# One common order of 63 steps between two attentions, rearranged

## The chip, the cores and the metric

The kernel runs on one core of a Trainium2 chip. A core has four compute engines that run side by side, each working through its own instruction queue in order: TensorE (PE, matrix products and transposes through the array), VectorE (DVE), ScalarE (ACT) and GpSimd (POOL). SyncE (SP) issues the DMAs. The engines meet only at semaphores: an instruction waits until a counter has reached a value, and everything behind it in its queue waits too. The metric is the device time of one execution in microseconds.

## The reference, cut to what matters

Two layers over 1024 tokens of width 512. Each computes `x + attention(norm(x)) * silu(ffn(norm(x)))`; the first layer's attention has 8 heads of 8 channels, its feed-forward part is a base product with eight low-rank experts. What concerns this case is the passage from the first layer's attention to the second's:

```
s  = attention_0(xn)            # ends in out @ Wo_w.T + Wo_b, per tile of 128 tokens
x  = x + s * g                  # g = silu(ffn_0(xn)), already there
xn = _layernorm(x)              # over the 512 channels
q = (xn @ Wq.T)                 # 32 heads of 128, 8 groups of 4 heads
k = (xn @ Wk.T); v = (xn @ Wv.T)   # 8 key/value heads of 128
q, k = _rmsnorm(q, q_norm_w), _rmsnorm(k, k_norm_w)
scores = q k^T / sqrt(128) + alibi bias, causal; softmax; @ v; @ Wo.T
```

## The kernel before

Tokens are handled in eight tiles of 128 rows. Products in full precision are made from three products of half-split operands (`mm3`, L2035 to L2039: high by high, high by low, low by high), so each operand of TensorE comes as a high part, mostly written by ScalarE, and a low part, mostly written by VectorE (what is left after the high part is taken away).

The program has three stages that matter here. First comes a loop of 32 steps of the first attention. Into its last steps tiles 0 to 3 of the next stage are woven (`EARLY = 4`). Then comes the stretch that this case is about, written out as a list of 63 steps, `TAIL` (L322 to L328). Then comes a long loop of 64 slots of the second attention (`slot_items`), which goes through the key/value groups one by one.

A step of `TAIL` is a pair (kind, tile). Four engines walk the same list, each doing its own share of a step (TensorE L2334, ScalarE L1322, VectorE L1815, GpSimd L1053); a step in which an engine has no share is passed over. SyncE doesn't walk it. The kinds are:

- `OS` and `OH`: TensorE transposes the attention sums of a tile (L2223), VectorE divides them (`normalise`, L1680 to L1691); TensorE transposes the result (L2230), ScalarE writes its high half (L1245), VectorE its low half (`low_on`, L1700).
- `WO`: TensorE makes the first layer's output product into bank WB (three matmuls, L2239 to L2243), VectorE multiplies it with the gate (L1708), GpSimd adds x (`add_x`, L1034). The sum is what SyncE stores (L784).
- `LS` and `LA`: statistics of the new x on VectorE (L1494, L1495), reciprocal root on GpSimd (`rstd`, L934 to L940), and the normalised tile on ScalarE (`apply_act`, L1320).
- `XT`: TensorE transposes the normalised tile (L2058), ScalarE and VectorE write the halves (L1137, L1507).
- `KV`: key/value product of a tile for group 0 (twelve matmuls of 256 columns, into the S banks), ScalarE squares the keys (L1338) and copies the values (L1340), GpSimd makes the inverse root (`inverse_k`, L962, L963). `VL` is VectorE's low half of the values (L1796), `SC` VectorE's scaling of the keys (L1806), `KT` the transpose of the keys (L2316) with its halves (L1304, L1777).
- `PQ`, `SQ`, `QT`: query projection of a row tile (twelve matmuls of 512 columns; `PQ` 0 goes to bank VB, `PQ` 1 to bank WB), sums of squares on ScalarE (L1279), inverse roots on GpSimd (`inverse_rms`, L955 to L957), scaling on VectorE (L1764), transposes (L2311) and halves (L1300, L1772).
- `S0`: the four score products of the first query tile, VectorE's bias and maximum (L1784), ScalarE's exponentials (L1310).

Semaphore values are computed from the list. The transposes of `OS`, `OH`, `XT`, `KT` and `QT` alternate between the two halves of bank T, so each waits until VectorE has emptied the one before last (`ring`). `KV` of tiles 4 to 7 waits until `VL` and `SC` of the tile four before are done (`KV_FREE`). `KV` of tiles 4 to 7 and `PQ` 1 wait for VectorE's half of `XT`; `OH` waits for its `OS` on VectorE; `QT` 1 waits for all sixteen `VL` and `SC` steps. The first work of slot 0 of the long loop is another query projection into WB, which waits for `SQ` 1, then the scores of its first head, which wait for every `KT` and `QT` of the list on VectorE.

Of the kernel before, what the change touches and what calls it, by code (L numbers as in the profile page):

```python
# [16 lines left out]
NT, KT = TOK // P, D // P  # L17
# [22 lines left out]
QT = 10240  # L40
# [180 lines left out]
def slot_items(n):  # L221
# [65 lines left out]
    else:  # L287
# [31 lines left out]
T_OUT = 16  # L319


TAIL = [("KV", 0), ("OS", 4), ("KV", 1), ("VL", 0), ("OH", 4), ("OS", 5), ("KV", 2), ("VL", 1), ("WO", 4),  # L322
# [6 lines left out]
KV_FREE = {}  # L329
for _x in TAIL:  # L330
    if _x[0] in ("VL", "SC"):
# [8 lines left out]
T_AT = {}  # L340
for _x in TAIL:
    if _x[0] in ("OS", "OH", "XT", "KT", "QT"):
# [125 lines left out]
def program(nc, x, w0, w1, codes, absmax, lora, consts, rows, rel, out):  # L468
    with ExitStack() as ctx:
# [451 lines left out]
        def _(pool):  # L921
# [8 lines left out]
            def rstd(t, bias=False):  # L930

                k = t % NT
                hold(pool, var_ready, t + 1, p_passed)
                ch.link(e.tensor_scalar(VE[:, k:k + 1], MV[:, k, 1:2], 1.0, LN_EPS, ALU.mult, ALU.add))  # L934
                root = e.tensor_tensor(RSTD[:, k:k + 1], VE[:, k:k + 1], C[:, C_EXP:C_EXP + 1], ALU.pow)
                if bias:

                    ch.link(root)
                    ch.link(e.tensor_tensor(NB[:, k:k + 1], MV[:, k, 0:1], RSTD[:, k:k + 1], ALU.mult))
                    root = e.tensor_scalar(NB[:, k:k + 1], NB[:, k:k + 1], -1.0, 0.0, ALU.mult, ALU.add)  # L940
                root.then_inc(rstd_ready, 1)
# [95 lines left out]
            for x in range(NBX):  # L1037
# [4 lines left out]
                for it in unit_items(x):  # L1042
# [8 lines left out]
                    elif it[0] == "LS":  # L1051
                        rstd(NT + it[1])
            for kind, t in TAIL:  # L1053
                if kind == "WO":
# [75 lines left out]
        def _(act):  # L1130
# [190 lines left out]

            for x in TAIL:  # L1322
                kind, b = x
# [163 lines left out]
        def _(dve):  # L1487
# [326 lines left out]

            for x in TAIL:  # L1815
                kind, t = x
# [215 lines left out]
        def _(pe):  # L2032
# [300 lines left out]

            for x in TAIL:  # L2334
                kind, b = x
# [301 lines left out]
```

## Time and profile before

| | us |
|---|---|
| median of 3 runs | 1408.86 (1408.39 to 1411.47) |
| the profiled execution's own time | 1408.48 |
| its span, first to last instruction | 1406.7 |
| mean granted TensorE clock, share of full speed | 0.989 |
| busy in the span: TensorE, VectorE, ScalarE, GpSimd | 1344.7, 931.9, 880.0, 660.8 |

The profile tells for each engine how long it was busy, and for each instruction what ended the idle time before it. Times of single instructions are counted from the span's start. Ends of matmuls are modelled, so that neighbouring matmuls overlap in the listing; the distance from start to start is what one costs in a row of them. Instructions are told by line: in this stretch L2037 to L2039 are products (bank S for `KV`, VB and WB for `PQ`), L2058 is `XT`, L2223 `OS`, L2230 `OH`, L2239 the start of `WO`, L2311 `QT` and L2316 `KT`.

### The profile page before, as it was taken

Reading aid. Unit: us, or ns where it says so; the run is one execution under the profiler, and the core shown is the slowest. Engines: PE = TensorE matmul, PEld = TensorE weight load, DVE = VectorE, ACT = ScalarE, POOL = GpSimd, SP = SyncE. Lnnn points to the kernel's source line nnn. Section 1 sums busy time; section 2 is a strip of 40 time slices with the busy share of each in tenths; the row PEclk is TensorE's granted clock in tenths of the full one; section 3 lists DMA queues with packets and bytes.
Section 4 is the critical chain, followed back from the end, with each engine's and each line's share of the span. In section 5 each row is a group of like instructions: output and inputs, shape, how many; then the busy total and the mean of one; then the engine's idle time right before and its main releaser. Section 6 shows DMA issues by size and latency. Waiting matters only on the chain. (4 is left out here: it accounts for less than half of the span.)

```text
span 1406.7 us, 21472 instructions
## 1 busy us (share of the span) xinstructions
PE 1344.7 (96%) x7350; PEld 1078.3 (77%) x7350; DVE 931.9 (66%) x1659; ACT 880.0 (63%) x2167; POOL 660.8 (47%) x988
## 2 busy tenths in 40 slices
PE   6898987999999999999999999999999999999997
PEld 5543345788888888888888888888888887778886
DVE  5766555667776777767677767777676777676433
ACT  6255564667776777667677767776676766663211
POOL 5233266445465555545454645555454545443311
PEclk9999999899999999999999999999999999999999
DMA  4100032102010110102020101101020202033110
GB/s 162 53 1 1 0 106 71 31 1 61 27 51 11 52 56 22 47 16 77 2 61 27 51 11 52 61 16 51 12 77 1 62 11 50 5 95 120 36 61 30
DMA packets 36028, 61.02 MB, mean 43 GB/s; under 512 B 9200, under 2 KB 13424, under 8 KB 35920
## 3 DMA queue, kind: packets, MB, share of 16 engines
q1 hardware_dynamic: 35920, 59.66, 13.6%
q8 instruction: 59, 0.97, 0.3%
q14 instruction: 49, 0.40, 0.1%
HBM read 49.68 MB, written 9.96 MB: 42 GB/s over the span
## 5 line engine op out<-in xcount | busy, mean ns | idle before, releaser
L947 POOL TENSOR_TENSOR RI<-SM,C 128x1 f32<-128x1 f32 x256 | 151.8, 593 | 410.3 <-ACT PB L1310 410.1
L1791 DVE TENSOR_TENSOR R<-T,R 128x512 fp32r<-128x512 f32 x288 | 198.8, 691 | 115.4 <-ACT R L1383 105.0
L1784 DVE CUSTOM_DVE_ANT_0 PB<-S,REL,SLC 128x128 f32<-128x128 f32 (+7 forms) x256 | 204.6, 813 | 82.9 <-PE S L2039 79.9
L1310 ACT ACTIVATE PB<-PB,NM 128x128 f32<-128x128 f32 (+7 forms) x256 | 198.2, 774 | 45.5 <-DVE NM L1784 44.7
L1383 ACT ACTIVATE R<-T 128x512 fp32r<-128x512 f32 x288 | 171.3, 596 | 81.1 <-PE T L2428 78.0
L948 POOL TENSOR_SCALAR PB<-PB,RI 128x128 f32<-128x128 f32 (+7 forms) x256 | 209.7, 819 | 25.2
L2428 PE MATMUL T<-C,PB 128*128 128x128 f32 x1152 | 176.0, 276 | 7.6 <-DVE R L1791 3.3
L2428 PEld LDWEIGHTS T<-C,PB 128*128 128x128 f32 x1152 | 135.7, 141 | 37.6 <-DVE R L1791 13.9
L1370 ACT ACTIVATE DQ<-DQ 128x704 f32<-128x704 int32 x128 | 97.5, 785 | 78.4 <-DVE DQ L1865 76.4
L2037 PE MATMUL WB<-R,XT 128*128 128x512 f32 (+1 forms) x268 | 105.1, 392 | 0.0
L2039 PE MATMUL WB<-R,XT 128*128 128x512 f32 (+1 forms) x268 | 103.9, 388 | 0.0
L2038 PE MATMUL WB<-R,XT 128*128 128x512 f32 (+1 forms) x268 | 103.7, 387 | 0.0
L2037 PE MATMUL T<-R 128*128 128x512 f32 x256 | 101.8, 398 | 1.0 <-DVE R L1791 1.0
L2039 PE MATMUL T<-R 128*128 128x512 f32 x256 | 100.4, 392 | 0.0
L2038 PE MATMUL T<-R 128*128 128x512 f32 x256 | 100.0, 391 | 0.0
L2037 PE MATMUL S<-R 128*128 128x512 f32 (+3 forms) x252 | 92.8, 368 | 0.9 <-DVE NM L1784 0.9
L1211 ACT ACTIVATE PB<-S 128x1024 f32<-128x1024 f32 x64 | 65.1, 1023 | 43.8 <-PE S L2186 43.5
L2039 PE MATMUL S<-R 128*128 128x512 f32 (+3 forms) x252 | 89.7, 356 | 0.0
L1279 ACT ACTIVATE JUNK<-WB 128x128 bf16<-128x128 f32 x252 | 65.5, 273 | 33.5 <-PE WB L2039 33.5
L1865 DVE TENSOR_TENSOR DQ<-DQ 128x704 f32<-128x704 f32 x96 | 86.4, 900 | 0.0
L2038 PE MATMUL S<-R 128*128 128x512 f32 (+3 forms) x240 | 84.9, 354 | 0.0
L1653 DVE TENSOR_REDUCE MH<-T 128x2 f32<-128x1024 f32 x48 | 58.8, 1225 | 35.5 <-PE T L2170 35.5
(311 smaller groups left out, 3501.9 us busy)
## 6 DMA issues: line engine op xcount, KB each, us to landing
RAW<-w SPq DMA_DIRECT2D x85, 256.0 KB, 2.7
DQ<-codes SPq DMA_DIRECT2D x16, 352.0 KB, 4.0
DQ<-absmax SPq DMA_DIRECT2D x16, 352.0 KB, 2.9
dequantised<-DQ SPq DMA_DIRECT2D x16, 352.0 KB, 4.1
PB<-dequantised SPq DMA_DIRECT2D x5, 512.0 KB, 3.5
PB<-x SPq DMA_DIRECT2D x8, 256.0 KB, 4.7
PB<-x_scratch SPq DMA_DIRECT2D x8, 256.0 KB, 3.7
out<-PB SPq DMA_DIRECT2D x8, 256.0 KB, 2.0
```

Source lines behind the costliest of these rows:

```text
L947: ch.link(e.tensor_tensor(RI[:, k:k + 1], SM[:, k:k + 1], C[:, C_EXP + 5:C_EXP + 6], ALU.pow))
L948: e.tensor_scalar(pb(m, a, 0, L), pb(m, a, 0, L), RI[:, k:k + 1], scale, ALU.mult, ALU.mult).then_inc(probs_ready, 1)
L1310: e.activation(pb(m, a, 0, L), pb(m, a, 0, L), ACT.Exp, scale=-1.0, bias=NM[:, k:k + 1], accum_out=SM[:, k:k + 1]).then_inc(exp_done, 1)
L1370: e.activation(DQ[:, to, :], CODES, ACT.Copy, scale=sc, bias=bi).then_inc(line, 1)
L1383: e.activation(r(PT + AT[i, ("PV", kb)] % 3 * 1024, 512), T[AT[known, it] % 2][:, :], ACT.Copy).then_inc(t_act, 1)
L1784: e.tensor_tensor_reduce(out=pb(m, a, 0, L), in0=bank[:, 0:L], in1=REL[:, TOK - L:TOK], scale=SLC[:, a:a + 1], scalar=3.0e38, op0=ALU.add, ...
L1791: e.tensor_tensor(r(o + 512, 512), bank[:, :], rf(o, 512), ALU.subtract).then_inc(t_free, 1)
L1865: e.tensor_tensor(DQ[:, b, :], DQ[:, b, :], DQ[:, 3, :], op).then_inc(line_used, 1)
L2037: e.matmul(dst, lh, rh, start=start, stop=False)
L2038: e.matmul(dst, lh, rl, start=False, stop=False)
L2039: return e.matmul(dst, ll, rh, start=False, stop=stop)
L2428: last = e.transpose(bank[:, a * P:(a + 1) * P], pb(i, a, kb * P, (kb + 1) * P), IDENT)
```

## The change

The list `TAIL` gets another order. It holds the same 63 steps. Nothing else is edited; the semaphore values and the places in bank T follow from the list.

```diff
-TAIL = [("KV", 0), ("OS", 4), ("KV", 1), ("VL", 0), ("OH", 4), ("OS", 5), ("KV", 2), ("VL", 1), ("WO", 4),
-        ("OH", 5), ("OS", 6), ("KV", 3), ("SC", 0), ("LS", 4), ("WO", 5), ("OH", 6), ("OS", 7), ("VL", 2),
-        ("SC", 1), ("KT", 0), ("LA", 4), ("LS", 5), ("WO", 6), ("OH", 7), ("SC", 2), ("KT", 1), ("XT", 4),
-        ("LA", 5), ("LS", 6), ("WO", 7), ("PQ", 0), ("VL", 3), ("SC", 3), ("KT", 2), ("XT", 5), ("LA", 6),
-        ("LS", 7), ("KV", 4), ("KT", 3), ("XT", 6), ("VL", 4), ("SQ", 0), ("LA", 7), ("KV", 5), ("SC", 4),
-        ("QT", 0), ("XT", 7), ("VL", 5), ("KT", 4), ("KV", 6), ("SC", 5), ("PQ", 1), ("KT", 5), ("KV", 7),
-        ("VL", 6), ("SC", 6), ("KT", 6), ("S0", 0), ("VL", 7), ("SC", 7), ("KT", 7), ("SQ", 1), ("QT", 1)]
+TAIL = [("OS", 4), ("OS", 5), ("OH", 4), ("KV", 0), ("WO", 4), ("OH", 5), ("OS", 6), ("SC", 0), ("KV", 1),
+        ("WO", 5), ("OH", 6), ("LS", 4), ("OS", 7), ("SC", 1), ("KV", 2), ("WO", 6), ("OH", 7), ("KT", 0),
+        ("LS", 5), ("VL", 0), ("VL", 1), ("LA", 4), ("KV", 3), ("KT", 1), ("WO", 7), ("VL", 2), ("LS", 6),
+        ("LA", 5), ("SC", 2), ("XT", 4), ("LS", 7), ("PQ", 0), ("XT", 5), ("VL", 3), ("KT", 2), ("SC", 3),
+        ("LA", 6), ("KV", 4), ("XT", 6), ("SQ", 0), ("SC", 4), ("KT", 3), ("LA", 7), ("KV", 5), ("VL", 4),
+        ("XT", 7), ("VL", 5), ("KV", 6), ("VL", 6), ("SC", 5), ("QT", 0), ("SC", 6), ("KT", 4), ("PQ", 1),
+        ("KT", 5), ("KT", 6), ("KV", 7), ("S0", 0), ("SQ", 1), ("SC", 7), ("VL", 7), ("QT", 1), ("KT", 7)]
```

## Rows read from the trace of the kernel before

**Rows 1.** The page, part 1: busy us (share of the span) xinstructions
```profile
PE 1344.7 (96%) x7350; PEld 1078.3 (77%) x7350; DVE 931.9 (66%) x1659; ACT 880.0 (63%) x2167; POOL 660.8 (47%) x988
```

**Rows 2.** Windows: length, busy time by engine, PEclk, DMA share, GB/s
```profile
204.30:245.40 41.10, 31.52 (x193) 26.12 (x189) 21.28 (x68) 18.92 (x72) 22.87 (x49) 0.93 0.25 85
218.00:222.70 4.70, 4.54 (x14) 3.37 (x15) 3.16 (x9) 1.30 (x2) 3.16 (x9) 0.64 0.15 56
243.00:250.00 7.00, 5.45 (x16) 4.44 (x16) 1.70 (x3) 1.05 (x2) 3.50 (x8) 0.51 0.22 67
...
265.00:1150.00 885.00, 881.86 (x4998) 750.11 (x4998) 626.36 (x1148) 629.65 (x1694) 454.60 (x728) 1.00 0.12 37
```

**Rows 3.** Timeline of PE, later part: start, length, operation, idle before
```profile
218.16 0.66 PE L2058 MATMUL T<-C,PB 128*128 128x128 f32 x4 [1.95 <-DVE R L1700]
...
233.85 0.40 PE L2037 MATMUL WB<-R,XT 128*128 128x512 f32 x1
...
236.61 0.27 PE L2316 MATMUL T<-C,L0S 128*128 128x128 f32 x1
...
244.62 1.09 PE L2311 MATMUL T<-C,QN 128*128 128x128 f32 x4 [1.55 <-issue]
245.36 0.78 PE L2037 MATMUL WB<-R,XT 128*128 128x512 f32 x1
...
250.36 0.40 PE L2037 MATMUL S<-R 128*128 128x512 f32 x1
...
259.87 0.80 PE L2311 MATMUL T<-C,QN 128*128 128x128 f32 x4 [1.99 <-DVE QN L1764]
```

**Rows 4.** Timeline of ACT
```profile
204.48 0.60 ACT L1232 ACTIVATE DQ<-VB 128x512 f32<-128x512 f32 x1 [0.70 <-PE VB L2199]
...
215.22 0.80 ACT L1320 ACTIVATE PB<-PB,NB,RSTD 128x512 f32<-128x512 f32 x1
...
224.29 0.28 ACT L1279 ACTIVATE JUNK<-VB 128x128 bf16<-128x128 f32 x1 [4.13 <-PE VB L2039]
```

**Rows 5.** Timeline of DVE
```profile
206.36 0.21 DVE L1680 RECIPROCAL RS<-T 128x8 f32<-128x8 f32 x1 [1.85 <-PE T L2223]
...
206.87 0.28 DVE L1796 TENSOR_TENSOR R<-S,R 128x128 fp32r<-128x128 f32 x1
...
210.62 0.69 DVE L1708 SCALAR_TENSOR_TENSOR G<-WB,G 128x512 f32<-128x512 f32 x1 [1.12 <-PE WB L2243]
...
243.78 0.68 DVE L1764 TENSOR_TENSOR QN<-WB,INV 128x512 f32<-128x512 f32 x1
```

**Rows 6.** Timeline of PE, the first 7 us of the stretch
```profile
203.34 1.06 PE L2199 MATMUL VB<-PB,L0S 128*32 128x512 f32 x8 [1.86 <-ACT PB L1211]
204.34 0.38 PE L2037 MATMUL S<-R,XT 128*128 128x256 f32 x1
...
205.87 0.38 PE L2223 MATMUL T<-C,DQ 128*128 128x128 f32 x2
...
209.36 0.49 PE L2239 MATMUL WB<-R 64*128 64x512 f32 x1
...
210.35 0.27 PE L2230 MATMUL T<-C,ON 128*128 128x128 f32 x1
```

**Rows 7.** Timeline of POOL, in the stretch and in the long loop
```profile
211.40 1.28 POOL L1034 TENSOR_TENSOR PB<-PB,G 128x512 f32<-128x512 f32 x1 [0.65 <-DVE G L1708]
...
213.71 0.19 POOL L934 TENSOR_SCALAR VE<-MV 128x1 f32<-128x1 f32 x1
...
215.04 1.28 POOL L1034 TENSOR_TENSOR PB<-PB,G 128x512 f32<-128x512 f32 x1
...
225.79 1.03 POOL L956 TENSOR_TENSOR SQC<-SQB,C 128x4 f32<-128x4 f32 x1
...
323.50 0.91 POOL L948 TENSOR_SCALAR PB<-PB,RI 128x768 f32<-128x768 f32 x1
...
325.01 1.29 POOL L948 TENSOR_SCALAR PB<-PB,RI 128x768 f32<-128x768 f32 x1
```

## The prediction, made before the changed kernel ran

> **What bounds the kernel now.** I read the page first: TensorE is busy 96% of the span, far above the others [rows 1]. Then the windows. In the long loop it is busy 881.9 of 885.0 us, so whatever reaches that loop earlier ends earlier by the same amount. In the stretch of the 63 steps it is busy only 31.5 of 41.1 us, its granted clock is 0.93 in the mean, in two parts of it (218 to 222.7, 243 to 250) it is 0.64 and 0.51, so that there TensorE ran at the lower of its two levels, 1.2 against 2.4 GHz, most or all of the time [rows 2]. No other engine is busy more than 23 us of the 41. So the stretch is bound by chains between in-order queues, not by an engine. Last I read the timelines for what ends each pause. TensorE's pauses add up to 41.1 - 31.5 = 9.6 us. The longest is 1.95 us ahead of `XT` 4: it waits for VectorE's `OH` 7 half, which stood behind a statistics step that waited for GpSimd. At the end it pauses 1.55 us ahead of `QT` 1, and the next query projection, at the half clock, runs from 245.36 to 250.36, 5.00 us, where the same twelve matmuls took 236.61 - 233.85 = 2.76 at the full one [rows 3]. ScalarE stood 4.13 us at `PQ` 0's squares with later key transposes queued behind them [rows 4].
>
> **The change, part by part.** No instruction, DMA or byte is added or removed; only waits and order differ. SyncE's queue isn't reordered; its stores follow GpSimd's additions, which come earlier or within 0.3 us of before for the last tiles. So the cost is found by walking the four queues in the new order, with each step's length from the rows and about 0.05 to 0.15 us from one engine to the next (transpose listed as ending at 206.25, division at 206.36) [rows 5, 6]. I walk to one point: the first score product of slot 0, 250.36 before [rows 3].
>
> *The front.* The list now opens with `OS`, `OS`, `OH` where two key/value products stood. The last values product ends at 204.40, and before, `KV` 0 began at 204.34, hiding the copy of the sums [rows 6]. Now TensorE must wait for that copy, which ends at 205.08 [rows 4]; `OS` 4 starts at 205.15. VectorE's division follows at 205.64 and is done about 0.6 later (its three instructions take 0.51 to the next one's start [rows 5], and the last ends a little after that), so `OH` 4 runs at 206.35 and `KV` 0 at 206.45, 2.1 us later than before. That is the loss. In exchange `WO` 4 starts at 206.45 + 1.53 = 208.0 and not at 209.36; a `KV` costs 205.87 - 204.34 = 1.53, a `WO` 210.35 - 209.36 = 0.99 [rows 6]. The gate (0.69) is done at 210.0 [rows 5] and GpSimd's first addition runs at 210.1, not 211.4 [rows 7].
>
> *The middle, TensorE.* From there it finds everything ready: `KV` 1 to 210.8, `WO` 5 to 211.9, `KV` 2 to 213.7, `WO` 6 to 214.7, `OH` 7 at 214.74, just as its division ends, `KV` 3 to 216.5, `WO` 7 to 217.6, `XT` 4 to 218.0, `PQ` 0 (2.76) to 220.7, `XT` 5 to 221.1, `KV` 4 to 222.9. The 1.95 us pause goes, since `XT` 4's bank is emptied by `OH` 7 and `KT` at about 216.2, before `LS` 5 in VectorE's queue.
>
> *The middle, GpSimd.* This is the next chain. An addition costs 1.28, the root of `LS` with its three small steps 215.04 - 213.71 = 1.33 [rows 7], a key root about 0.8 (estimated: an `LS` root without two of its small steps). `LS` 4 can start when the second addition ends, 214.3, and from there GpSimd never rests: `LS` 4, root, addition 6 to 217.7, `LS` 5 to 219.1, root, addition 7 to 221.1, `LS` 6 to 222.6, `LS` 7 to 223.9, `PQ` 0's roots (1.03 for the long one, 1.6 in all [rows 7]) to 225.4. ScalarE applies each in 0.80 [rows 4]. So `XT` 6 waits until 223.55 (0.45 of listed pause), and `XT` 7, whose ScalarE step stands behind `KT` 3's half, until 225.85 (0.15). `SQ` 0 ends at 226.2, long before `QT` 0 is due at 227.8. ScalarE's 4.13 us wait goes too: when it comes to `PQ` 0's squares, after `XT` 4, it waits at most 0.5.
>
> *The end.* `KV` 6 to 227.8, `QT` 0, `PQ` 1 to 231.1, `KV` 7 to 232.9, two first scores to 233.6, the other two 0.35 later each as VectorE frees their banks. VectorE's four maxima, of 128 columns like the 0.28 of a `VL` [rows 5] and with a result to read back, end at about 235.1, `SQ` 1 (0.68 [rows 5]) at 235.8, `SC` 7 and `VL` 7 at 236.3. `QT` 1 waits for these: listed pause 1.95, start 236.4. `KT` 7 now stands last and is ready for 0.1. Slot 0's projection starts at 237.0, where 245.36 stood, and at the full clock its score product starts at 237.0 + 2.76 = 239.8. GpSimd's first probabilities are ready at 238.5 and all at 241.5, before the transposes that need them (244).
>
> *The sum.* 250.36 - 239.8 = 10.6 us. It comes out again another way. New listed pauses: 0.75 + 0.70 at the front, 0.1 at `KT` 2, 0.45, 0.15, 0.2 at the scores and 1.95, together 4.3 against 9.6: 5.3 less. Some seven pauses fewer also spare the end of a matmul that is otherwise overlapped (listed 0.40, but 2.76/12 = 0.23 from start to start [rows 3], so 0.16 each): 1.1. The half clock between 218 and 222.7, 0.36 of 4.7 us below full and so 0.72 of it at half [rows 2], cost some 1.7, and with the small steps up to 1.9, and the one at slot 0's projection 2.24. 5.3 + 1.1 + 1.9 + 2.2 = 10.5.
>
> *The clock, the unknown term.* In the trace it was low behind the 1.95 us pause and around the 1.55 us one [rows 2, 3]. The new order has two such places: the front (1.86 us before the last values product [rows 6], then 0.75 and 0.70) and the end (0.2, then 1.95). Bounds: nothing where it stays up; 2.24 each where it falls and stays down over a whole query projection, as before [rows 3]. I take one fall of the two, 1.9: 10.5 - 1.9 = 8.6. The later pause of 1.99 us in slot 0 [rows 3] is taken as it was. The Trainium skill speaks against the change at the front: "TensorE: Matmul & The Clock Gate", section on what is actually happening, has the engine throttled by default and the full rate only granted for recent activity, so a front of short transposes and waits should lose it. By that rule both falls come and the gain is about 6.8; the trace agrees that the clock falls behind clustered pauses, yet after the 1.86 us pause ahead of the last values product `KV` 0 ran at 0.13 us a matmul, the full rate [rows 6].
>
> *Against the profiled execution.* Its own time, 1408.48, is 0.38 below the median of 1408.86. 1408.5 - 8.6 = 1399.9; I forecast 1400.0.
>
> **The rivals.** *A: GpSimd becomes the bound (20%).* It works back to back from 214.3 to 225.4. The same scaling in the long loop took 0.91 and, 1.5 us later, 1.29 [rows 7]: 0.38 more. If each of the seven long steps of the chain grows so, `LA` 6, `LA` 7 and all after come 2.5 us later; with one clock fall the gain is 6.1, and with both, 4.2: 1402.4 to 1404.3. For: the stretch packs VectorE denser beside it. Against: both additions listed in the stretch took 1.28 [rows 7]. The Trainium skill, "SBUF — State Buffer", section "Who interferes with whom", has a VectorE instruction with two SBUF inputs block a GpSimd one that reads SBUF. Nearly all VectorE steps here read PSUM for one input, so by that rule little would be added; the row agrees.
>
> *B: the clock stays up more than I grant (12%).* Neither fall comes, or the transposes behind slot 0's 1.99 us pause, listed at 0.80 and so probably at the half clock [rows 3], run with what follows at the full one, worth up to 1.7 more as the fall above: gain 10.5 to 12.2, 1396.3 to 1398.
>
> *C: slower, by the half clock (5%).* The clock falls at the front, at 205, and the short pauses keep it down to the end of the stretch. At the half clock a 512-column matmul costs 0.42 (5.00/12) against 0.23, so each us of full-speed work costs 0.8 more. The 10.5 us gain is used up from 13 us of such work on; over all of the stretch's 27 us (31.5 less overlapped ends and slow parts) it is 22 - 10.5: 1420. For: three pauses in 5 us at the front. Against: both falls in the stretch ended once TensorE issued without pause, and from 206.45 to 221.1 it has none.
>
> *D: no change (5%).* The waits that follow from the list hold the ends where they were, or slot 0 waits for something else that doesn't move (its chunks of weights, the probabilities): within 2.8 us. Against: the weights for slot 1 are issued after GpSimd's last low halves, which move with the rest.
>
> **The numbers.** Forecast 58%, own range 1398.0 to 1402.4. With 12% below that, 20% above in A, 5% no change, 5% slower. The range for 8 in 10 is 1396.3 to 1404.3. A measurement of this kernel can tell about 0.2%, 2.8 us: faster 0.90, same 0.05, slower 0.05.
>
> **What would show it right or wrong.** In the new profile: two short pauses ahead of L2223 and L2230 at 204.4 to 206.4; the first L1034 of the stretch near 210.1; no pause over 0.5 us on TensorE from 207 to 223; GpSimd without rest from 214 to 225; a pause of about 2 us ahead of the last L2311; slot 0's first score product at 239.8 to 242. The walk is wrong if that product comes later than 244 with the clock at full, or if TensorE pauses over 1 us in the middle. The gain should stand whole at the end of the span: if the score product comes 8 us earlier and the end doesn't, the claim about the long loop is what failed.

## The result, and the profile after

The changed kernel takes 1398.25 us (median of 4 executions, 1396.86 to 1399.49) against 1410.03 for the kernel before in the same rounds: ratio 0.9917, 95% interval 0.9900 to 0.9935. The forecast was 1400.0, range 1396.3 to 1404.3. Over the executions whose clock was recorded the kernel before has a mean of 1410.5 (60 executions; two more, of 2189.89 and 2638.86, are far out of line and left out) and the changed one 1399.6 (10): 10.9 us, give or take 2.2. The profiled execution took 1399.04, its span is 1397.2.

The profile's page, first part, then windows of the stretch: length, busy time by engine, PEclk (the clock granted to TensorE, as a share of full speed), DMA share, GB/s. The first window runs from the last values product to slot 0's query projection and answers to the first of [rows 2]:

```profile
PE 1342.4 (96%) x7350; PEld 1075.9 (77%) x7350; DVE 933.1 (67%) x1659; ACT 880.2 (63%) x2167; POOL 661.8 (47%) x988
```

```profile
205.50:239.90 34.40, 30.12 (x193) 25.64 (x189) 21.20 (x67) 18.42 (x71) 20.40 (x44) 0.95 0.25 90
206.50:210.50 4.00, 3.57 (x18) 3.07 (x18) 1.38 (x7) 0.28 (x1) 0.00 (x0) 0.57 0.45 182
210.50:239.90 29.40, 26.36 (x172) 22.44 (x172) 19.63 (x59) 17.54 (x69) 20.40 (x44) 1.00 0.20 67
...
255.00:1150.00 895.00, 891.98 (x5044) 758.03 (x5043) 635.39 (x1163) 637.11 (x1712) 461.57 (x738) 1.00 0.12 37
```

The stretch is 34.4 us and not 41.1, with the same 193 matmuls in the window; TensorE's listed pauses are 34.4 - 30.1 = 4.3 us and not 9.6. The half clock (1.2 GHz) comes once, at the front, between 206.5 and 210.5. In the long loop TensorE is as full as before.

TensorE's timeline, with all its pauses from the last values product to slot 0's transposes (it answers to [rows 3, 6]):

```profile
204.53 1.06 PE L2199 MATMUL VB<-PB,L0S 128*32 128x512 f32 x8 [1.77 <-ACT PB L1211]
206.41 0.78 PE L2223 MATMUL T<-C,DQ 128*128 128x128 f32 x4 [0.81 <-ACT DQ L1232]
207.62 0.45 PE L2230 MATMUL T<-C,ON 128*128 128x128 f32 x1 [0.43 <-DVE ON L1691]
207.75 0.55 PE L2037 MATMUL S<-R,XT 128*128 128x256 f32 x1
...
210.42 0.50 PE L2239 MATMUL WB<-R 64*128 64x512 f32 x1
...
226.25 0.63 PE L2058 MATMUL T<-C,PB 128*128 128x128 f32 x4 [0.62 <-DVE R L1777]
...
228.62 0.63 PE L2058 MATMUL T<-C,PB 128*128 128x128 f32 x4 [0.20 <-ACT PB L1320]
...
236.60 0.33 PE L2037 MATMUL S<-R 128*128 128x128 f32 x1 [0.27 <-DVE NM L1784]
...
239.34 0.66 PE L2311 MATMUL T<-C,QN 128*128 128x128 f32 x4 [1.85 <-DVE R L1796]
...
239.86 0.47 PE L2037 MATMUL WB<-R,XT 128*128 128x512 f32 x1
...
242.70 0.39 PE L2037 MATMUL S<-R 128*128 128x512 f32 x1
...
252.19 0.66 PE L2311 MATMUL T<-C,QN 128*128 128x128 f32 x4 [1.99 <-DVE QN L1764]
```

The 1.95 us pause ahead of `XT` 4 is gone, and so are those ahead of `QT` 0 and of four key transposes, of 0.80 to 1.22 us (three of these five show below, in the kernel with the old rest of the list). The row at 226.25 names VectorE's half of `KT` 2, which ends at 226.16; `XT` 6 needs ScalarE's `LA` 6, which ends at 226.11 (row below). Slot 0's projection takes 242.70 - 239.86 = 2.84 us (5.00 before). From the end of the last values product (205.59; 204.40 before) to slot 0's first score product it is now 37.11 us and was 45.96. The span shrank by 9.5: 8.85 here, 1.84 behind it (1156.34 us from that score product to the end before, 1154.50 now), less 1.19 ahead of the stretch, which the list doesn't touch.

Of the 1.84 us, 1.59 lie in slot 0. Its 1.99 us pause is there in both, but before, the clock fell at it (0.84 from 259.8 to 270.4 us, 1.00 in the 9 us ahead of that) and now it doesn't (1.00 from 252.1 to 262.7). TensorE's timeline at the next group of such transposes (`L2311`) behind that pause, of the kernel before, then of the changed one:

```profile
278.92 0.60 PE L2311 MATMUL T<-C,QN 128*128 128x128 f32 x4
```

```profile
269.67 0.60 PE L2311 MATMUL T<-C,QN 128*128 128x128 f32 x4
```

From slot 0's first score product that is 278.92 - 250.36 = 28.56 us before and 269.67 - 242.70 = 26.97 now; I call this place "past slot 0's fall".

### The profile page after: what moved, and what is told of

Its sections match the earlier page's. It is cut to its first block and busy times, and to the rows that moved or that the text cites. A ratio compares the mean times of both kernels' runs of the same rounds, so it can differ in the third digit from the quotient of the medians.

```text
span 1397.2 us, 21472 instructions
## 1 busy us (share of the span) xinstructions
PE 1342.4 (96%) x7350; PEld 1075.9 (77%) x7350; DVE 933.1 (67%) x1659; ACT 880.2 (63%) x2167; POOL 661.8 (47%) x988
## 5 line engine op out<-in xcount | busy, mean ns | idle before, releaser
L2428 PEld LDWEIGHTS T<-C,PB 128*128 128x128 f32 x1152 | 135.7, 141 | 37.8 <-DVE R L1791 13.6
L2037 PE MATMUL WB<-R,XT 128*128 128x512 f32 (+1 forms) x268 | 103.9, 388 | 0.0
L2039 PE MATMUL WB<-R,XT 128*128 128x512 f32 (+1 forms) x268 | 103.0, 384 | 0.0
L2038 PE MATMUL WB<-R,XT 128*128 128x512 f32 (+1 forms) x268 | 102.6, 383 | 0.0
```

The source lines that it names most:

```text
L2037: e.matmul(dst, lh, rh, start=start, stop=False)
L2038: e.matmul(dst, lh, rl, start=False, stop=False)
L2039: return e.matmul(dst, ll, rh, start=False, stop=stop)
L2428: last = e.transpose(bank[:, a * P:(a + 1) * P], pb(i, a, kb * P, (kb + 1) * P), IDENT)
```

## The experiments

All are timed in rounds with the kernel before. I write "equal clock" for what is left of a difference in time when the clock's part is taken out, as below. To compare places in the trace I use distances from the end of the last values product (`L2199`), since that end itself lies between 202.6 and 210.5 us from one execution to the next. In us, by the profiled execution of each kernel:

| | first `WO` | `PQ` 0 | `QT` 1 | first score of slot 0 | past slot 0's fall |
|---|---|---|---|---|---|
| before | 4.96 | 15.71 | 40.22 | 45.96 | 74.52 |
| changed | 4.83 | 14.72 | 33.75 | 37.11 | 64.08 |
| changed, once more | 3.75 | 13.64 | 32.67 | 37.50 | 64.51 |
| old head, new rest | 4.96 | 15.71 | 35.63 | 40.44 | 67.39 |
| new head, old rest | 4.85 | 14.77 | 38.41 | 43.41 | 70.39 |
| end alone | 4.96 | 15.44 | 39.27 | 44.14 | 71.08 |
| `LS` 5 later | 5.91 | 15.25 | 40.72 | 46.61 | 75.15 |
| front filled | 3.75 | 13.63 | 32.66 | 37.33 | 64.28 |
| both filled | 3.74 | 13.63 | 32.70 | 36.04 | 64.57 |
| `KV` 0 first | 4.38 | 13.44 | 32.46 | 37.21 | 64.17 |
| the same, end filled | 4.37 | 13.46 | 32.47 | 35.81 | 64.37 |
| `PQ` 1 early | 4.35 | 13.44 | 34.87 | 40.07 | 67.05 |
| before, filled | 4.97 | 15.35 | 38.66 | 41.88 | 70.43 |

The last column stands behind every place where these profiles show the half clock in or just after the stretch, so it holds what the order and its falls of the clock give together: 74.52 - 64.08 = 10.4 us for the change (10.0 in its repeat).

Every execution has its mean granted clock. Over all of them one line fits with a spread of 1.03 us: a constant for each kernel, less 1.04 us for each 0.001 of clock. It parts what the order gives at one and the same clock from what the clock gives; but the mean clock is that of the whole kernel, and most of its spread comes from ahead of the stretch (last section), so a difference in mean clock between two kernels is not all the list's:

| | executions | mean us | mean clock | at clock 0.990 |
|---|---|---|---|---|
| before | 60 | 1410.5 | 0.9876 | 1408.0 |
| before, filled | 12 | 1407.0 | 0.9903 | 1407.3 |
| end alone | 10 | 1406.0 | 0.9911 | 1407.1 |
| `LS` 5 later | 10 | 1409.6 | 0.9871 | 1406.6 |
| new head, old rest | 10 | 1406.4 | 0.9886 | 1405.0 |
| `PQ` 1 early | 12 | 1403.9 | 0.9909 | 1404.8 |
| old head, new rest | 4 | 1400.5 | 0.9925 | 1403.1 |
| front filled | 6 | 1399.2 | 0.9920 | 1401.2 |
| changed | 10 | 1399.6 | 0.9915 | 1401.2 |
| `KV` 0 first, end filled | 6 | 1399.2 | 0.9918 | 1401.1 |
| both filled | 6 | 1399.0 | 0.9918 | 1400.9 |
| `KV` 0 first | 6 | 1397.7 | 0.9927 | 1400.5 |

### The two halves of the list

```diff
 # old head: the old list up to ("WO", 7), the rest in the new order
+        ("LA", 5), ("LS", 6), ("WO", 7), ("LS", 7), ("PQ", 0), ("XT", 5), ("VL", 3), ("KT", 2), ("SC", 3),
...
 # new head: the new list up to ("WO", 7), the rest in the old order
+        ("LS", 5), ("VL", 0), ("VL", 1), ("LA", 4), ("KV", 3), ("KT", 1), ("WO", 7), ("VL", 2), ("SC", 2),
+        ("XT", 4), ("LA", 5), ("LS", 6), ("PQ", 0), ("VL", 3), ("SC", 3), ("KT", 2), ("XT", 5), ("LA", 6),
...
```

> The old list up to WO 7 (30 steps), the other 33 steps in the new list's order. Measured from the end of the last values product to slot 0's first score product, before took 45.96 us and the changed kernel 37.11. Theory (the pauses in the chains add up by place): this half holds the pauses ahead of QT 0, KT and QT 1, so the tail alone saves about 4.9 us of waits and 2.2 of half clock: about 7 us faster than before (39 us in the stretch), with the 1.95 us pause ahead of XT 4 still there. Rival (the head decides, since GpSimd's additions start everything): 2 us or less. Second rival (only the clock counts): 2.2 us, and the pauses listed in TensorE's timeline stay near 9.6 us.

> The new list up to WO 7 (25 steps), the other 38 steps in the old list's order: the complement of the run with the old head. Theory: about 2 us faster than before (3.5 if the clock stays up at the front), the pause ahead of XT 4 gone, those ahead of QT 0, the key transposes and QT 1 (0.84, 1.22, 0.80, 0.91, 1.55 us) still there, and the half clock at slot 0's projection with them or not by the phase. The two halves together should give the whole 8.9 us of the stretch. Rival (the head decides): 6 us or more.

Measured: 1400.69 us (ratio 0.9934, 0.9908 to 0.9959) and 1405.27 (0.9968, 0.9947 to 0.9989). TensorE's timeline of the kernel with the old head, ahead of `XT` 4, `QT` 1, slot 0's projection and first score product; then that of the kernel with the new head, ahead of `QT` 0, two key transposes and `QT` 1:

```profile
220.08 0.66 PE L2058 MATMUL T<-C,PB 128*128 128x128 f32 x4 [1.94 <-DVE R L1700]
...
241.95 1.11 PE L2311 MATMUL T<-C,QN 128*128 128x128 f32 x4 [1.85 <-DVE R L1796]
...
242.93 0.77 PE L2037 MATMUL WB<-R,XT 128*128 128x512 f32 x1
...
246.76 0.39 PE L2037 MATMUL S<-R 128*128 128x512 f32 x1
```

```profile
230.28 0.66 PE L2311 MATMUL T<-C,QN 128*128 128x128 f32 x4 [0.84 <-DVEq L1813]
...
232.59 0.30 PE L2316 MATMUL T<-C,QN 128*128 128x128 f32 x1 [1.22 <-DVE R L1772]
...
239.47 0.33 PE L2316 MATMUL T<-C,L0S 128*128 128x128 f32 x1 [0.79 <-DVE L0S L1806]
...
245.13 1.09 PE L2311 MATMUL T<-C,QN 128*128 128x128 f32 x4 [1.54 <-issue]
```

Each pause stays with its half. Up to `QT` 1 the old head with the new rest saves 40.22 - 35.63 = 4.59 us, the new head 1.81, together 6.40, and the whole change 6.47. They add up in these profiles; an interaction smaller than one fall of the clock, which alone moves that point by 1.1 us from one execution to the next, could hide in this. Past slot 0's fall they give 7.13 and 4.13 us, and the whole 10.44. Neither the head alone (rival) nor the clock alone (rival) carries the gain. Seven tenths of it up to `QT` 1 lie in the second half. Against what was expected: to slot 0's first score product the halves save 5.52 and 2.55 us, 8.07 together for the 8.85 of the whole; in time at equal clock 4.9 and 3.0, for about 7 and 2. In the profile with the old head the clock was low for part of slot 0's projection (246.76 - 242.93 = 3.83 us), so the 2.2 us of that term came in part.

### The end alone, and one step moved

```diff
-        ("VL", 6), ("SC", 6), ("KT", 6), ("S0", 0), ("VL", 7), ("SC", 7), ("KT", 7), ("SQ", 1), ("QT", 1)]
+        ("VL", 6), ("SC", 6), ("KT", 6), ("S0", 0), ("SQ", 1), ("SC", 7), ("VL", 7), ("QT", 1), ("KT", 7)]
```

> The old list with its last six steps alone in the new order (S0, SQ 1, SC 7, VL 7, QT 1, KT 7). Theory: SQ 1 follows the four maxima and no longer KT 7's round through ScalarE, QT 1 at 39.1 us after the last values product and not 40.2: 1.1 us; slot 0's score product 1.1 to 3.3 us earlier, by the clock. Rival (the end of the list is what the whole change lives from): 4 us or more. Rival (nothing: QT 1 waits for the same last key step either way): 0.

```diff
-        ("SC", 1), ("KT", 0), ("LA", 4), ("LS", 5), ("WO", 6), ("OH", 7), ("SC", 2), ("KT", 1), ("XT", 4),
+        ("SC", 1), ("KT", 0), ("LA", 4), ("WO", 6), ("OH", 7), ("SC", 2), ("KT", 1), ("LS", 5), ("XT", 4),
```

> The old list with one step moved: LS 5 from ahead of WO 6 to behind KT 1. Theory (the 1.95 us pause ahead of XT 4 is OH 7's low half behind a statistics step that waits 0.65 us for GpSimd and then takes 0.83): the pause shrinks to about 0.9 us, PQ 0 starts 14.6 us after the last values product and not 15.7, and the half clock behind it may go, worth up to 1.7 more at XT 5. Rival (the pause belongs to WO 6 and the gate, which VectorE would wait for anyway): XT 4's pause within 0.3 us of 1.95.

Measured: 1406.33 (ratio 0.9968, 0.9952 to 0.9984) and 1408.73 (1.0005, 0.9987 to 1.0023). The end alone brings `QT` 1 0.95 us forward and 0.9 us at equal clock: its theory, to 0.2 us. To the score product it is 1.82 us, within the 1.1 to 3.3. The ratio says more, 4.5 us, since these executions had a mean clock of 0.9911. With `LS` 5 later the pause ahead of `XT` 4 is

```profile
224.10 0.66 PE L2058 MATMUL T<-C,PB 128*128 128x128 f32 x4 [0.89 <-DVE R L1700]
```

in place of 1.95 [rows 3]: the cause of that pause is settled. The time is a half hit. At equal clock it is 1.4 us faster, but these executions had a mean clock of 0.9871, and the timed ratio shows nothing; in the profiled one the first `WO` came at 5.91 and not 4.96, so `PQ` 0 came at 15.25, not 14.6, and slot 0's projection ran at the half clock as before (score product at 46.61, 45.96 before). What a single step gives is below what these rounds can show without the clock beside each time.

### The clock: idle matmuls in the pauses

```diff
+            def fill(n, bank):
+                for _ in range(n):
+                    e.matmul(bank, r(W_H, P), r(W_H, 512), start=True, stop=True)
...
+                if x in (("OS", 4), ("OH", 4)):
+                    fill(3, S[1][:, 512:1024])
+                if x == ("QT", 1):            # in the kernel with both filled
+                    fill(8, VB[:, :])
```

> The changed kernel with three idle 512-column matmuls into a free bank ahead of OS 4 and three more ahead of OH 4, where TensorE pauses 0.81 and 0.43 us; nothing reads them. Theory (the half clock behind these pauses, 3.4 us of it, costs 1.2 us or more, since GpSimd's first addition hangs on WO 4): the clock stays at full, KV 0 takes 1.5 us and not 2.7, and the stretch is 1.2 us shorter than the changed kernel's 37.1; where the fill itself is late it costs at most 0.3. Rival (the clock at the front is hidden under GpSimd's chain): no change of the point where slot 0's score product starts. Second rival: the clock falls anyway.

> The changed kernel with idle matmuls into free banks in both places where TensorE rests: three of 512 columns each ahead of OS 4 and OH 4, and eight ahead of QT 1. Theory (a pause costs more than itself only through the clock): QT 1 at 32.7 us after the last values product as with the front filled alone, slot 0's score product 2.8 to 3.0 us after the projection's start since the clock stays up, 36.1 in all against 37.3; the median 0.5 to 1.5 us under the changed kernel's 1398.25. Rival (eight idle matmuls delay QT 1 by as much as they save): no change from the run with the front filled.

> The changed kernel once more, unchanged, on the chip and in the rounds of these two, to have its time and clock over more executions. Expected: median 1397.5 to 1399.5, mean clock 0.992.

Measured: 1398.16 (ratio 0.9924, 0.9898 to 0.9950), 1398.31 (0.9928, 0.9907 to 0.9949), and 1400.43 (0.9915, 0.9890 to 0.9941) for the unchanged repeat. The front of the filled kernel, and the front of the repeat without any fill:

```profile
208.20 1.07 PE L2199 MATMUL VB<-PB,L0S 128*32 128x512 f32 x8 [1.74 <-ACT PB L1211]
209.20 0.96 PE L2337 MATMUL S<-R 128*128 128x512 f32 x3
210.08 0.63 PE L2223 MATMUL T<-C,DQ 128*128 128x128 f32 x4
210.46 0.94 PE L2337 MATMUL S<-R 128*128 128x512 f32 x3
211.29 0.30 PE L2230 MATMUL T<-C,ON 128*128 128x128 f32 x1
...
213.02 0.49 PE L2239 MATMUL WB<-R 64*128 64x512 f32 x1
```

```profile
211.27 0.63 PE L2223 MATMUL T<-C,DQ 128*128 128x128 f32 x4 [0.81 <-ACT DQ L1232]
212.49 0.30 PE L2230 MATMUL T<-C,ON 128*128 128x128 f32 x1 [0.59 <-DVE ON L1691]
...
214.21 0.49 PE L2239 MATMUL WB<-R 64*128 64x512 f32 x1
...
243.13 1.12 PE L2311 MATMUL T<-C,QN 128*128 128x128 f32 x4 [1.85 <-DVE R L1796]
...
247.96 0.39 PE L2037 MATMUL S<-R 128*128 128x512 f32 x1
```

In both, at the full clock, `WO` 4 starts 3.75 us after the last values product, and all up to `QT` 1 is 1.08 us earlier than in the first profile of the changed kernel (32.67 against 33.75): this is the price of one fall at the front, in the point that matters, so GpSimd's chain doesn't hide it. But the repeat had the full clock there with no fill at all, and then the half clock at slot 0's projection (247.96 - 243.13 is 4.83 us from `QT` 1 to the score product, 3.36 in the first profile). One and the same kernel's clock falls at the front in one execution and at the end in another. So two filled profiles with the clock up at the front don't show that the fill there holds it. And the stretch as a whole was not 1.2 us shorter with the front filled: the clock was low at slot 0's projection, and the score product came at 37.33. Over the executions the filled kernels have a mean clock of 0.9920 and 0.9918, the unfilled one 0.9915: no difference that these numbers can carry.

The fill at the end is another matter. The both-filled kernel had slot 0's score product at 36.04, as expected, 2.8 us after the projection's start. The same holds in all three profiles with eight or six idle matmuls ahead of `QT` 1, and in only one of the ten others, the first of the changed kernel; in the nine left it took 3.7 to 5.2 us. But in all three the clock then fell behind slot 0's 1.99 us pause. TensorE's timeline past slot 0's fall, both filled:

```profile
273.49 0.60 PE L2311 MATMUL T<-C,QN 128*128 128x128 f32 x4
```

That is 273.49 - 244.96 = 28.53 us after the score product, and 26.94 to 27.01 in the eight profiles where the clock stays up there. So the fill at the end saves 1.1 to 1.5 us at the projection and 1.6 are lost in slot 0: past slot 0's fall the both-filled kernel is at 64.57, the front-filled one at 64.28, the changed one at 64.08 and 64.51. In these profiles the fall was moved, not spared, and the median of 0.5 to 1.5 us under the changed kernel's didn't come (1398.31 for 1398.25). The repeat's own median missed its 1397.5 to 1399.5 too, by 0.9.

> The old list unchanged, with idle 512-column matmuls into bank VB where TensorE rests: eight ahead of XT 4 (pause 1.95 us), three each ahead of KT 4, KT 6 and KT 7, six ahead of QT 1 (1.55 us). Nothing reads them. Over all runs so far the time of every kernel falls by about 1 us for each 0.001 of mean granted clock, and before has 0.988 where the changed kernel has 0.992. Theory (a third of the 11 to 12 us that the change gives is half clock that no longer comes, and only the order's pauses bring it): with the pauses filled the mean clock of before rises to 0.991 or 0.992 and its median falls 3 to 5 us, to 1404.5 to 1406.5, with QT 1 still 38.5 to 40.3 us after the last values product. Rival (the lower clock comes from elsewhere in the kernel, by the phase of each execution): clock stays 0.988, time within 1 us of before. Rival (the idle matmuls delay more than they save): slower.

```diff
+                if x == ("XT", 4):
+                    fill(8, VB[:, :])
+                if x in (("KT", 4), ("KT", 6), ("KT", 7)):
+                    fill(3, VB[:, :])
+                if x == ("QT", 1):
+                    fill(6, VB[:, :])
```

Measured: 1406.52 (ratio 0.9966, 0.9946 to 0.9986). The fill in place of the 1.95 us pause, and `QT` 1:

```profile
218.83 2.09 PE L2337 MATMUL VB<-R 128*128 128x512 f32 x8
221.02 0.66 PE L2058 MATMUL T<-C,PB 128*128 128x128 f32 x4
...
245.91 0.63 PE L2311 MATMUL T<-C,QN 128*128 128x128 f32 x4 [0.15 <-issue]
```

With the old order and most of its waits, work that nobody reads makes the kernel faster: by 5.1 us in the medians, 3.6 in the means over all executions (give or take 2.3); the mean clock goes from 0.9876 to 0.9903. At equal clock hardly anything is left (0.7). The place can be seen in the profile: from the last values product to slot 0's first score product the mean clock is 1.00 for 0.89 before, and the time 41.88 us for 45.96. The fall in slot 0 is there in both, so the 4.1 us stay to the end. The theory's 3 to 5 us holds within the noise (its 1404.5 to 1406.5 and 0.991 just missed). The rival that the low clock comes from elsewhere falls for this difference, though not for the spread between executions of one kernel.

### Other orders

```diff
-TAIL = [("OS", 4), ("OS", 5), ("OH", 4), ("KV", 0), ("WO", 4), ("OH", 5), ("OS", 6), ("SC", 0), ("KV", 1),
+TAIL = [("KV", 0), ("OS", 4), ("OS", 5), ("OH", 4), ("KV", 1), ("WO", 4), ("OH", 5), ("OS", 6), ("SC", 0),
```

> The changed kernel with KV 0 moved ahead of OS 4 and KV 1 ahead of WO 4, so that one covers the copy of the sums and the other the wait for OH 4's low half. Theory: pause at the front 0.7 us and not 1.24, clock stays up, WO 4 starts about 4.2 us after the last values product (4.8 in the changed kernel) and WO 5 right behind it, so GpSimd's chain from the second addition on starts 2 us earlier and slot 0's score product comes 1.5 to 2.3 us earlier than in the changed kernel. Rival (TensorE's own work is the bound once the clock is up): 0.5 to 1.2 us. Rival (WO 4 first matters, as the new list has it): no gain or a loss up to 0.6.

> The order of the run with KV 0 first, with eight idle matmuls ahead of QT 1. Theory: QT 1 at 32.5 us after the last values product, slot 0's first score product at 35.8 in every execution, median 1396 to 1397.4, the best so far, mean clock 0.993 or more. Rival: the median stays at the 1397.35 to 1398.3 of the other versions, the rest of the kernel's clock deciding.

Measured: 1397.35 (ratio 0.9917, 0.9891 to 0.9942) and, with the end filled too, 1399.70 (0.9910, 0.9891 to 0.9929). Against the changed kernel at the full clock, `QT` 1 comes 0.21 us earlier (32.46 against 32.67); the 1.29 against its first profile are for the rest the clock. The theory of 1.5 to 2.3 us fell, and even the 0.5 of the first rival was too much; the second (no gain) is the nearest. `WO` 4 is 0.6 us later (4.38 for 3.75), and `WO` 5, which should have followed at once, finds bank WB still with VectorE's gate; TensorE's timeline at `WO` 5:

```profile
209.52 0.50 PE L2239 MATMUL WB<-R 64*128 64x512 f32 x1 [0.53 <-DVE G L1708]
```

So it starts only 0.2 us earlier than in the changed kernel, a new wait in place of the old one, and that 0.2 is what arrives. With the end filled, slot 0's score product came at 35.81 as expected, but the clock then fell in slot 0 (past its fall 64.37, and 64.17 without the fill), and the median of 1396 to 1397.4 didn't come. At equal clock the 0.7 us to the changed kernel is less than the spread of 1.03 with six executions can tell for sure. It is not shown to be better, only not worse.

```diff
-        ("XT", 7), ("VL", 5), ("KV", 6), ("VL", 6), ("SC", 5), ("QT", 0), ("SC", 6), ("KT", 4), ("PQ", 1),
-        ("KT", 5), ("KT", 6), ("KV", 7), ("S0", 0), ("SQ", 1), ("SC", 7), ("VL", 7), ("QT", 1), ("KT", 7)]
+        ("XT", 7), ("PQ", 1), ("VL", 5), ("SC", 5), ("QT", 0), ("KV", 6), ("KT", 4), ("KV", 7), ("SQ", 1),
+        ("VL", 6), ("SC", 6), ("KT", 5), ("S0", 0), ("VL", 7), ("SC", 7), ("KT", 6), ("QT", 1), ("KT", 7)]
```

> The order of the run with KV 0 first, and in its last part the second query projection PQ 1 set right behind XT 7, ahead of KV 6, so that its squares, roots and scaling (about 3.6 us from its end to SQ 1's end) run under KV 6, KV 7 and S0 and no longer under KV 7 and S0 alone. Theory (the 1.85 us pause ahead of QT 1 is this chain plus SC 7 and VL 7 behind S0): that pause shrinks to 0.6 us or less, QT 1 comes about 1.3 us earlier than in the run with KV 0 first (31.1 us after the last values product, 32.46 there), slot 0's first score product about 34.5 at the full clock: the best version so far, near 1395.5. Rival (SC 7 and VL 7 hang on KV 7's own squares and root, and S0's maxima stand ahead of them): QT 1 within 0.4 us of 32.46.

Measured: 1403.58 (ratio 0.9964, 0.9947 to 0.9980), 6 us slower than the version that it was built on (4.3 at equal clock, 2.9 past slot 0's fall in the profiles); `QT` 1 at 34.87 and not 31.1. The pause ahead of `QT` 1 did shrink, to 0.78, but two others came. TensorE's timeline ahead of `PQ` 1 and ahead of the third head of `S0`, then ScalarE's and VectorE's just before the latter:

```profile
226.54 0.50 PE L2037 MATMUL WB<-R,XT 128*128 128x512 f32 x1 [1.62 <-DVE XT L1507]
...
235.65 0.33 PE L2037 MATMUL S<-R 128*128 128x128 f32 x1 [1.91 <-DVE NM L1784]
```

```profile
233.48 1.15 ACT L1237 ACTIVATE R<-RAW 128x512 fp32r<-128x512 f32 x2
234.51 0.37 ACT L1304 ACTIVATE R<-T,QKW 128x128 fp32r<-128x128 f32 x1
```

```profile
234.91 0.35 DVE L1777 SCALAR_TENSOR_TENSOR R<-T,QKW,R 128x128 fp32r<-128x128 f32 x1 [0.94 <-ACT R L1304]
235.24 0.35 DVE L1784 CUSTOM_DVE_ANT_0 PB<-S,REL,SLC 128x128 f32<-128x128 f32 x1
```

`PQ` 1 right behind `XT` 7 waits for its halves on ScalarE and VectorE, a round that `KV` 6 covered. And `KT` 5 now stands behind `KV` 7, whose share on ScalarE brings two weight chunks (1.15 us); VectorE waits for `KT` 5's half with `S0`'s maxima queued behind. I had walked the chain of `PQ` 1 and not these two.

## Why the prediction was right, step by step

**The front: right.** Pauses 0.81 and 0.43 (0.59 in the repeat) for 0.75 and 0.70 forecast; at the full clock `WO` 4 at 3.75 us for 3.6 (208.0 less 204.4) and GpSimd's first addition at 5.8 for 5.7.

**The middle: right.** In the repeat, at the full clock, `PQ` 0 comes at 13.64 where the walk had 13.6 (218.0 less 204.4). No pause from the front to `XT` 6. GpSimd's timeline in the first profile: the first two additions of the stretch, the second of which opens the chain, and rows from the chain up to `PQ` 0's roots (it answers to [rows 7]):

```profile
212.45 1.28 POOL L1034 TENSOR_TENSOR PB<-PB,G 128x512 f32<-128x512 f32 x1 [0.65 <-DVE G L1708]
...
215.30 1.28 POOL L1034 TENSOR_TENSOR PB<-PB,G 128x512 f32<-128x512 f32 x1 [0.65 <-DVE G L1708]
216.67 0.19 POOL L934 TENSOR_SCALAR VE<-MV 128x1 f32<-128x1 f32 x1
...
225.34 0.19 POOL L934 TENSOR_SCALAR VE<-MV 128x1 f32<-128x1 f32 x1
...
227.06 1.02 POOL L956 TENSOR_TENSOR SQC<-SQB,C 128x4 f32<-128x4 f32 x1
```

From 215.30 it works without a rest of over 0.1 us to the end of `PQ` 0's roots at 228.4, 13.1 us, as walked (212.95 to 225.4, 12.5). ScalarE's `LA` 6 and its transposes show what that chain costs TensorE, 0.62 and 0.20 us for 0.45 and 0.15 forecast. ScalarE's 4.13 us wait [rows 4] is 0.36:

```profile
223.35 0.28 ACT L1279 ACTIVATE JUNK<-VB 128x128 bf16<-128x128 f32 x1 [0.36 <-PE VB L2039]
...
225.30 0.81 ACT L1320 ACTIVATE PB<-PB,NB,RSTD 128x512 f32<-128x512 f32 x1
```

Rival A had these steps growing; the additions are at the 1.28 us that they had.

**The end: right.** 0.27 and 1.85 for 0.2 and 1.95; `QT` 1 at 32.67 for 32.0 at the full clock. So the walk of four queues through 63 steps was off by 0.7 us in 32.

**The long loop: right.** From slot 0's score product to the end it is 1153.2 to 1157.8 us in the twelve profiles other than before's, and 1156.34 there, with no trend by the time of arrival.

**The sum, and the clock as the term that was mis-sized.** The terms for waits and uncovered ends, 5.3 + 1.1 = 6.4 us, stand: at equal clock the change is worth 1408.0 - 1401.2 = 6.8 us, give or take 0.8. For the clock the forecast took the half clock of before as its one profile had it (1.9 and 2.24 us), gave the changed kernel one fall of 1.9 in the stretch, and left the fall in slot 0 "as it was": 2.2 us net. The profiles show one fall in the stretch, as forecast, in the first at the front and in the repeat at the end; at the front it costs 1.08 us and not 1.9. To slot 0's first score product this makes 8.85 us, and 8.46 in the repeat, for 8.6. What the sum left out is the fall in slot 0: it came before (28.56 us) and came in neither profile of the changed kernel (26.97 and 27.01), 1.6 us more, the second half of rival B. With it the profiles give 10.4 and 10.0, and the means over all executions 10.9, give or take 2.2. The mean clocks say the same less sharply: 0.9876 to 0.9915 is worth 4.1 us, give or take 1.8, where I had 2.2. Why the clock stays up in slot 0 after the new list is not shown; in the one other unfilled profile where it fell there, with `LS` 5 later, slot 0's projection had run at the half clock throughout, as before (5.16 and 5.00 us).

That the number lies so near has luck in it. By the medians of the same rounds the change gave 11.8 us, by the ratio's interval 9.2 to 14.1, and 8.6 is under both. The forecast of 1400.0 was counted from an execution of 1408.48 with a clock of 0.989, better than the 1410.0 of the rounds and the 1410.5 of the mean, and that made up for about half of the 3.2 us by which its gain was too small.

**The rule on the clock** that I weighed against the change ("TensorE: Matmul & The Clock Gate" of the Trainium skill, the section on what is actually happening: throttled by default, released by activity) agrees with the trace in direction: behind the bunched pauses at the front the clock was 0.57 between 206.5 and 210.5 us, and 1.00 from there on, where TensorE worked without a pause to `XT` 6. It doesn't tell how many falls come. In the first profile the clock fell at the front and not at the end, in the repeat the other way round, and in neither at both, as the case of 6.8 us had it.

## What to carry to other kernels

Where all engines walk one written order, walk each queue with durations from the trace: it gave the arrival of `QT` 1 within 0.7 us in 32, and told which step hides which. A step's share on every engine counts, as the version with `PQ` 1 early showed: its gain on one chain was lost on two that weren't walked. Where TensorE pauses in bunches, a shorter pause can be worth more than itself, and the clock's part has to be taken from several executions, each time beside its granted clock, and not from one profile. And a fall of the clock that is held off in one place can come at the next pause, so the gain is to be read behind that pause.

## What the runs showed of the hardware that was not expected

One line fits 152 executions of twelve kernels: 1.04 us for each 0.001 of mean granted clock, with a spread of 1.03 us. The kernel before alone goes from 1406 at 0.991 to 1419.5 at 0.981. Much of that comes from ahead of the stretch. In the thirteen profiles the last values product ends between 202.6 us (mean clock 0.98 up to there) and 210.5 us (0.94), where the kernels don't differ. In the first 150 us the clock was 0.97 in the profile of before, 0.95 in the first of the changed kernel and 0.91 in its repeat, with the same program up to there. Windows (length, PE busy, PEclk, DMA share, GB/s) of the first changed profile, then of the repeat:

```profile
0.00:150.00 150.00, 125.18 (x650) 0.95 0.15 51
```

```profile
0.00:150.00 150.00, 124.59 (x625) 0.91 0.15 51
```

And idle matmuls, which nothing reads, made an unchanged order 3.6 us faster in the mean, while in the changed order those at the end only went with a fall in slot 0's pause in place of one at its projection (two profiles), and gained nothing that could be measured.
